# Weighted-value rounds in pairs at slots 2, 9 and 17 of a batch, and a ring of ten exponential tiles

## The reference

```python
x = x + tanh(g_xattn[0]) * L0_xattn(layernorm(x), ctx, ctx)      # 16 heads of 8, softmax over 154 keys
x = x + tanh(g_ffn[0])   * L0_ffn(layernorm(x))                  # quantised feed-forward, scales by the maximum of all of x
x = x + tanh(g_xattn[1]) * L1_xattn(layernorm(x), ctx, ctx)      # the same, causal
x = x + tanh(g_ffn[1])   * L1_ffn(layernorm(x))                  # c = f*c + i*g over the 4 batches, then tanh
```

```python
attn = softmax(q @ k.T / sqrt(8)); out = (attn @ v) @ Wo.T + bo   # per batch and head
```

## Time and profile before

| what | value |
|---|---|
| median of 3 runs | 403.72 us (400.42 to 404.03) |
| profiled execution, its own time | 402.88 us |
| span of the profile | 401.1 us |
| mean granted clock of TensorE | 0.868 of 2.4 GHz |

### The profile page before, as it was taken

One profiled execution on the slowest core, in us unless ns is written; L12 is line 12 of the kernel. 1 busy time (PEld: TensorE's weight loads), 2 busy tenths in 40 slices (PEclk: granted clock), 3 DMA queues, 4 the chain that ended last, 5 costly groups with the idle time before them and its releaser, 6 DMA issues. The chain is left out here.

```text
span 401.1 us, 4558 instructions
## 1 busy us (share of the span) xinstructions
PE 303.2 (76%) x1440; PEld 180.0 (45%) x1440; DVE 261.2 (65%) x600; ACT 187.8 (47%) x305; POOL 142.9 (36%) x270
## 2 busy tenths in 40 slices
PE   0867799999898638964600557887999989999975
PEld 0644554454433223422400555665566655454534
DVE  4668655977924848769998933876588585333504
ACT  1571356555476304598770282005745545663222
POOL 8698260660133010000698884005234404030110
PEclk9978579999999857996565598859999999999989
DMA  8702001020000000000000002200202000000003
GB/s 227 277 2 78 8 32 54 2 86 8 0 7 2 0 0 1 0 0 0 2 1 0 0 0 83 89 7 2 87 6 85 7 2 7 2 0 2 0 1 105
DMA packets 9808, 12.75 MB, mean 32 GB/s; under 512 B 920, under 2 KB 5400, under 8 KB 9784
## 3 DMA queue, kind: packets, MB, share of 16 engines
q1 hardware_dynamic: 9352, 12.00, 8.6%
q10 hardware_dynamic: 432, 0.47, 0.5%
HBM read 4.27 MB, written 1.05 MB: 13 GB/s over the span
## 5 line engine op out<-in xcount | busy, mean ns | idle before, releaser
L1073 DVE TENSOR_REDUCE sb_nm<-ps_top 128x2 f32<-128x308 f32 (+1 forms) x240 | 102.1, 483 | 41.8 <-PE ps_top L785 28.0
L656 ACT ACTIVATE sb_pr<-ps_score 128x512 f32<-128x512 f32 (+1 forms) x160 | 90.7, 585 | 80.7 <-PE ps_score L816 36.7
L785 PE MATMUL ps_top<-sb_Kd,sb_Q 128*128 128x308 f32 (+1 forms) x240 | 83.4, 409 | 11.6 <-DVE sb_nm L1073 6.1
L785 PEld LDWEIGHTS ps_top<-sb_Kd,sb_Q 128*128 128x128 f32 x240 | 50.5, 217 | 35.2 <-DVE sb_nm L1073 20.4
L531 POOL TENSOR_SCALAR sb_var<-sb_mv 128x4 f32<-128x4 f32 x16 | 3.9, 243 | 170.4 <-DVE sb_mv L1036 170.2
L813 PE MATMUL ps_score<-sb_Q,sb_Kd 128*128 128x512 f32 x128 | 61.9, 494 | 3.4 <-ACT sb_pr L656 2.0
L813 PEld LDWEIGHTS ps_score<-sb_Q,sb_Kd 128*128 128x128 f32 x128 | 24.9, 198 | 37.5 <-ACT sb_pr L656 27.6
L843 PE MATMUL ps_pv<-sb_pr,sb_V 128*32 128x512 f32 x256 | 34.1, 605 | 0.0
L764 PE MATMUL ps_misc<-sb_consts,sb_xn 128*128 128x128 f32 x64 | 12.5, 329 | 28.0 <-DVE sb_xn L1048 19.9
L434 POOL TENSOR_TENSOR sb_K<-sb_kf,sb_kh 128x308 fp32r<-128x308 f32 x8 | 9.2, 1158 | 49.7 <-ACT sb_kf L598 48.3
L548 POOL TENSOR_SCALAR sb_xn<-sb_xr,sb_nmean,sb_rstd 128x128 f32<-128x128 f32 x52 | 23.3, 460 | 1.4
(11 more groups left out here) (157 smaller groups left out, 574.0 us busy)
## 6 DMA issues: line engine op xcount, KB each, us to landing
sb_Q<-sb_qh SPq DMA_DIRECT2D x16, 256.0 KB
sb_Q<-sb_ql SPq DMA_DIRECT2D x8, 256.0 KB
sb_xr<-x SPq DMA_DIRECT2D x4, 256.0 KB, 8.2
out<-sb_xr SPq DMA_DIRECT2D x4, 256.0 KB, 2.7
sb_wsb<-w SPq DMA_DIRECT2D x1, 704.0 KB, 8.7
sb_wf<-wffn SPq DMA_DIRECT2D x1, 576.0 KB, 9.0
sb_wkr<-wkr SPq DMA_DIRECT2D x2, 256.0 KB, 7.4
sb_Q<-sb_nmT SPq DMA_DIRECT2D x16, 32.0 KB
```

The lines of the kernel that those rows point to most:

```text
L656: act.activation(pr[:, k % PRING, q0:T], score[k % SRING][:, q0:T], ACT.Exp, scale=SCALE).then_inc(exp_r, 1)
L785: ins = pe.matmul(cols, Q4[n % 3][:, g, P * qt:P * qt + P], Kd[n % 3][:, g, j:j + heads, 0:keys], start=True, stop=not masked, skip_group_ ...
L1073: dve.tensor_reduce(nm[:, qt, h0:h0 + heads], top[k % MRING][:, 0:keys * heads].rearrange("p (h k) -> p h k", h=heads), AX.X, ALU.max, neg ...
```

## The change

`PE_PLAN` gets other slots for the rounds, and the ring of exponential tiles grows from 8 to 10. Before, the tail rounds of the batch before stand in slots 1 and 3 and the rounds in slots 7, 10, 13 and 17. After it both tail rounds stand in slot 2, rounds 0 and 1 in slot 9 (behind the output projection of slot 8), rounds 2 and 3 in slot 17. The plans of ScalarE and VectorE are unchanged. No instruction is added or removed.

```diff
-PRING = 8
+PRING = 10
...
-PE_PLAN = [(1, "tail0", -1), (3, "tail1", -1), (4, "pre", 2), (6, "q", 2), (7, "round0", 0), (8, "wo", -1),
-           (10, "round1", 0), (13, "round2", 0), (14, "top", 1), (16, "post", -1), (17, "round3", 0),
+PE_PLAN = [(2, "tail0", -1), (2, "tail1", -1), (4, "pre", 2), (6, "q", 2), (8, "wo", -1), (9, "round0", 0),
+           (9, "round1", 0), (14, "top", 1), (16, "post", -1), (17, "round2", 0), (17, "round3", 0),
```

## The result

The changed kernel took 416.94 us (median of 4 runs, 416.45 to 418.55) against 403.77; the ratio is 1.0353, 95% interval 1.0291 to 1.0415. A second series of it gave 416.80 and 1.0316 (1.0281 to 1.0350). So it is slower, as forecast, but by 13 us and not by 5.5: outside the stated range. The profiled execution took 418.55 us with a span of 416.8.

What follows compares the result with a forecast made beforehand. VectorE was taken to pace slots 18 to 12, so pairs cost what it lacks beside them. Layer 0 +3.4 and layer 1 +2.1 gave +5.5 us, forecast 409 us (chance 0.60), range 401.5 to 412.5.

Steps and rivals of the forecast that it cites:

- What bounds the kernel: Slots 18 to 12: VectorE paces, TensorE at most three maxima ahead; a round costs nothing while VectorE has work queued.
- rival 1: TensorE is the bound after all; 22 mergings gain 0.34 us each, 7.5 us, so 396; chance 0.13.
- Place A: Slot 17, rounds 2 and 3: VectorE's gap of 0.84 grows, +0.86 us per batch; slots 13 to 17 shorten 0.2 or 0.35.
- Place B: Slot 2, both tail rounds: +1.7 and +0.8 us in layer 0's second and third batch, +0.6 in both of layer 1.
- Place C: Slot 9, rounds 0 and 1 behind the output projection: VectorE waits +0.3 us in layer 0, +0.8 in layer 1.
- the short gaps that go when round 0 leaves slot 7: VectorE's gaps ahead of the residual vanish because the projection comes earlier: -0.45 and up to -0.6 us.
- The step that failed: Batch windows were read at granted clock 1.00 (2.4 GHz), second and third of layer 0 at 24.17 and 22.73 us.
- the first batch of each layer: No projection or residual in layer 0's, maxima lag but catch up: -0.2 us; layer 1's +0.4 - 0.35 = 0.
- The last batch of layer 1: TensorE busy 25.38 of 25.91 us; three mergings give back 1.0, ScalarE's gaps take some 0.9: -0.1 us.
- Layer 0's last batch: No maxima, ScalarE's exponentials pace it; a pair starves ScalarE about 0.6 us and later work follows: +0.5 us.
- Rival 3: Pairs also starve ScalarE; slots behind each wait another 0.25 us, adding 4.5 us: 413; chance 0.08.
- The ring: Ten exponential tiles cost and gain nothing themselves; they avoid a wait worth at most 0.6 us a batch.

Runs made afterwards that it cites:

- Three one-place kernels: Kernel before with ring of ten and one pair only: tail rounds in slot 2 (412.10 us), rounds 0 and 1 in slot 9 (405.74), rounds 2 and 3 in slot 17 (408.46).
- the moved pair: Changed kernel with both tail rounds in slot 1 instead of slot 2, beside the statistics of slot 0: 415.08 us, ratio 1.0273.
- pair_r23: Kernel before with ring of ten and only rounds 2 and 3 paired in slot 17: 408.46 us, ratio 1.0127.
- The pair alone: Kernel before with ring of ten and only the two tail rounds paired in slot 2: 412.10 us, ratio 1.0209.
- this pair alone: Kernel before with ring of ten and only rounds 0 and 1 paired in slot 9: 405.74 us, ratio 1.0047.
- the repeats: Changed kernel with maxima's matmuls in slots where TensorE waits issued three times (413.24 us; with more slots 414.16) or twice (412.36, again 411.46).
- twofold repeats: Changed kernel with maxima's matmuls issued twice in third batches (slots 3 to 8) and layer 0's second (1 to 8): 412.36 us, again 411.46.
- the control with the same repeats: Kernel before with each maximum's matmul of the same slots issued twice: 405.16 us, ratio 1.0043.
- the last version: Kernel before with ring of ten and round 3 moved to slot 0 of the next batch for each layer's first two batches only: 404.05 us, ratio 1.0004.

## Why the prediction was right and wrong

**What bounds the kernel.** Right. VectorE paces slots 18 to 12, and each block of TensorE counts by what VectorE has beside it. Three one-place kernels and the moved pair show it, and rival 1 (22 x 0.34 us gained) is out. The rule of the Trainium skill ("TensorEngine Tiling (Array Packing)", Key Properties) that a change of tiling mode drains TensorE is not disproved by that: pairs do take 1.92 us against two times 1.07. The saving is real and lies where it is worth nothing. For the sentence of the Trainium skill on PSUM evacuation (the same page, PSUM Bottleneck) the prediction names the gap of 0.84 us. That gap does not speak for it: there VectorE waits for TensorE.

**Place A.** Forecast: the gap grows from 0.84 to 1.7; measured 1.71. That slots 13 to 17 give back only 0.2 to 0.35: TensorE's wait of 0.69 us at L799 bears it out, and so do the second batches of pair_r23 (+0.58 and +0.50).

**Place B.** 1.7 forecast and 1.77 measured in layer 0's second batch, 0.8 and 0.85 more (1.76 for 0.91) in its third, 0.6 and 0.64 in layer 1's second, and 0.5 more in layer 1's third. The pair alone cost less than forecast where VectorE had slack behind it (layer 1's second batch, no growth), more where the clock fell.

**Place C.** 0.3 forecast and 0.23 measured in layer 0, 0.8 and 0.69 in layer 1, at full clock. What I booked as a gain, the short gaps that go when round 0 leaves slot 7, was to leave a net 0.15 us in the second batch of layer 0; with this pair alone nothing came of it (24.13 for 24.17). The same move takes TensorE's work out of the slots in which it waits, and this the sum did not price.

**The step that failed.** "[...] the second and third batch of layer 0 as 24.17 and 22.73 us [...] all at a granted clock of 1.00": I read it and let it stand for the changed kernel, and every duration of the sum was taken at the upper level. The change takes rounds out of the slots in which TensorE waits for VectorE and puts them together elsewhere. TensorE's waits became more (1.18, 1.23 and 0.57 us within 6 us, for 0.25 and 1.24), and the granted clock fell to 1.2 GHz in the third batches; then the projection and the pair, which are the parts VectorE waits for, ran wholly or partly at the lower level (the pair 2.78 us instead of 1.92). That is why TensorE's busy time rose in those two batches. No term and no rival had this; it is worth 5.0 to 6.4 of the 13 us. That the repeats take the stretches away, in none of six third batches instead of eight of eight, shows that it hangs on how active TensorE is. It does not show where the limit lies: pair_r23 had a stretch behind the waits of the kernel before. The Trainium skill describes such a fallback in "TensorE: Matmul & The Clock Gate", in the section on HAM oscillation: a kernel whose TensorE waits between bursts of matmuls falls back to the slow level and starts the next burst there. Its case is a wait for DMA; here the waits are for VectorE, and the longest is 1.23 us. The trace agrees in that the stretches at 0.51 and 0.50 follow waits. It does not agree that each wait is followed by one: the changed kernel waited 1.15 us at 74.85 and ran the pair behind it at full clock. I had not used it.

**The size without the clock.** 6.7 to 8.1 us measured against 5.5 forecast; 411.9 would still have been inside the range. The batches at full clock: second of layer 0 +1.73 (forecast about 1.8), second of layer 1 +0.92 (about 0.7), third of layer 0 with twofold repeats +1.8 against the kernel before and +1.27 against the control with the same repeats (24.53, 22.73, 23.26), where about 1.3 were forecast. Against that control the six batches with maxima grew by 6.2 us together, where the terms of the sum give 5.1. The term that is off is the first batch of each layer: -0.2 and 0 forecast, since the maxima would catch up, +0.63 and +0.55 measured. The gap of place A stands in them like in the others; the row at 68.10 in the earlier trace rows lies in layer 0's first batch. The last batch of layer 1 gave +0.28 for -0.1. Layer 0's last batch was forecast at +0.5: up to its tail pair it was +0.76 in the second execution of the changed kernel (17.90 for 17.14). From there to layer 1 the two executions of the changed kernel differ by 2.0 us (135.39 and 137.39), and I did not take that apart.

**Rival 3** (ScalarE starved) plays a small part: in layer 1's last batch TensorE waited 1.5 us for exponentials instead of 0.9.

**The ring.** Right, nothing; whether eight tiles would have hurt the paired kernel was not tried.

## What to carry to other kernels

Merging blocks on one engine saves its switching cost but lengthens the time in which it feeds nobody; count for each block what the other engine has queued beside it, by place, and put the block where a long job stands there. When work is moved away from slots in which TensorE waits, ask what its clock does then: read how close the stage already is to long waits, and price the matmuls behind them at the lower level as a case of its own. An order that looks untidy, with single rounds strewn between waits, can be what keeps the clock up: here no third batch of such a kernel lost it in twelve, and each of eight did with the rounds in pairs.

## What was not expected of the hardware

That more work made the kernel faster: some 40 needless matmuls took 3.7 to 5.5 us off the changed kernel (416.9 to 413.2 and 411.5). The price of the lower level depends on what it meets: the stretch of 3.4 us on a tail pair made VectorE's gap 3.42 us instead of 1.77. The stretches did not stay at one place: in the two executions of the changed kernel that were looked at they began at 109.9 and at 104.5 us, while the order of instructions was the same. The waits alone do not decide either: behind the same waits, 0.25 and 1.23 or 1.24 us, TensorE kept full clock in the kernel before and lost it in pair_r23. And the times of one kernel go with the clock: beside the last version the kernel before took 400.67 us at a mean granted clock of 0.874 and 405.56 at 0.860.
